# A wait-driven attention and feed-forward kernel: one load queue, a split transform, folds behind the first slots, norms on three engines, flat scans

## The reference, cut to what matters

```python
# x: (8, 128, 256), ctx: (8, 128, 256), T = 128 steps, C = 256 channels
def step(carry, kv_t):                    # _wkv, scanned over the 128 steps
    p, q, o = carry
    no = jnp.maximum(o, u + kt); A = jnp.exp(o - no); E = jnp.exp(u + kt - no)
    y = (A * p + E * vt) / (A * q + E)
    ...                                   # p, q decay by exp(w) and take in exp(kt)*vt, exp(kt)
x = x + jnp.tanh(g_xattn[0]) * _wkv(w, u, _layernorm(x), ctx)
h = fwht(_layernorm(x) * SU_ug) / 64      # Walsh-Hadamard transform over 256
h = silu(h @ W_gate.T * s_gate) * (h @ W_up.T * s_up)         # inner width 1024
h = fwht(h * SU_dp) / 64                  # over 1024
x = x + jnp.tanh(g_ffn[0]) * (h @ W_down.T * s_dp)
```

## Time and profile before

| | before |
|---|---|
| time, median of 3 runs | 117.35 us (116.47 to 118.0) |
| time of the profiled execution | 116.77 us |
| its span, first to last instruction | 115.0 us |
| TensorE busy | 98.3 us, 85% |
| VectorE, ScalarE, GpSimd busy | 70.3, 67.5, 61.4 us |
| TensorE's share of the chain that ended last | 71% |
| mean granted TensorE clock | 0.996 |

### The profile page before, as it was taken

The page is one execution under the profiler, slowest core; times in us unless marked ns, Lnnn a source line. Parts: engine busy times, 40 slices in busy tenths (PEclk is TensorE's granted clock), DMA queues, the critical chain, the costliest instruction groups (busy, mean ns, idle before and its releaser), DMA issues.

```text
span 115.0 us, 1940 instructions
## 1 busy us (share of the span) xinstructions
PE 98.3 (85%) x684; PEld 88.9 (77%) x684; DVE 70.3 (61%) x145; ACT 67.5 (59%) x146; POOL 61.4 (53%) x76
## 2 busy tenths in 40 slices
PE   0027778899799999999999999999999999779990
PEld 0026555756489969699999999999999999679870
DVE  0399899908996795997996475972219611322211
ACT  4299675044699907999525899373659723405400
POOL 7022999799759897942432734624402542312420
PEclk9999999999999999999999999999999999999998
DMA  3899998000000000000000020000020000020002
GB/s 65 267 324 415 418 404 350 0 0 3 3 6 0 0 0 0 0 0 6 0 0 3 6 91 0 0 0 0 6 91 0 3 0 6 0 91 0 3 1 90
DMA packets 3036, 7.62 MB, mean 66 GB/s; under 512 B 465, under 2 KB 850, under 8 KB 2898
## 3 DMA queue, kind: packets, MB, share of 16 engines
q1 hardware_dynamic: 2880, 7.48, 17.7%
q10 hardware_dynamic: 146, 0.02, 0.1%
HBM read 6.45 MB, written 1.05 MB: 65 GB/s over the span
## 4 chain that ended last, share of the span: by engine, by line
PE 71%; DVE 15%; ACT 4%; DMA 4%; issue 2%; POOL 1%; POOLq 1%; DVEq 0%; ACTq 0%
PE UG L899 38%; PE OD L937 12%; PE KZ L937 6%; PE UG L826 5%; PE FX L858 5%; DMA X<-in_x 4%; DVE X L327 2%; PE FX L867 2%; DVE BS L667 1%; DVE XT L761 1%; PE VB L875 1%; DVE SP_ L639 1%; DVE SQ L639 1%; ACT S L595 1%; DVE DEN L697 1%
## 5 line engine op out<-in xcount | busy, mean ns | idle before, releaser
L458 POOL TENSOR_TENSOR HL<-H,HH 128x256 fp32r<-128x256 f32 x32 | 25.8, 814 | 32.3 <-ACT HH L586 32.3
L775 DVE SCALAR_TENSOR_TENSOR H<-S,ALPHA,UG 128x256 f32<-128x256 f32 x32 | 15.0, 478 | 22.3 <-ACT S L595 22.2
L595 ACT ACTIVATE S<-UG,VT 128x256 f32<-128x256 f32 x32 | 15.1, 473 | 17.5 <-PE UG L899 17.5
L899 PE MATMUL UG<-FH,WTH 128*128 128x256 f32 x128 | 21.4, 289 | 0.8 <-ACT FH L580 0.8
L899 PE MATMUL UG<-FL,WTH 128*128 128x256 f32 x128 | 20.4, 281 | 0.0
L899 PE MATMUL UG<-FH,WTL 128*128 128x256 f32 x128 | 20.3, 280 | 0.0
L899 PEld LDWEIGHTS UG<-FH,WTH 128*128 128x128 f32 x128 | 17.8, 188 | 2.1 <-issue 1.9
L899 PEld LDWEIGHTS UG<-FH,WTL 128*128 128x128 f32 x128 | 17.4, 188 | 0.0
L899 PEld LDWEIGHTS UG<-FL,WTH 128*128 128x128 f32 x128 | 17.3, 188 | 0.0
L586 ACT ACTIVATE HH<-H 128x256 fp32r<-128x256 f32 x32 | 13.2, 413 | 4.5 <-DVE H L775 4.2
L937 PE MATMUL OD<-HH,MH 128*128 128x256 f32 x40 | 11.3, 283 | 1.6 <-DVE XT L761 1.6
(11 more groups left out here) (120 smaller groups left out, 200.3 us busy)
## 6 DMA issues: line engine op xcount, KB each, us to landing
WN<-in_weights SPq DMA_DIRECT2D x4, 512.0 KB, 9.1
DN<-in_w_down SPq DMA_DIRECT2D x1, 1024.0 KB, 8.1
out<-XT SPq DMA_DIRECT2D x3, 256.0 KB, 2.5
V<-in_ct SPq DMA_DIRECT2D x2, 258.0 KB, 7.7
V<-in_ct SPq DMA_DIRECT2D x1, 516.0 KB, 12.1
X<-in_x SPq DMA_DIRECT2D x2, 256.0 KB, 4.7
XT<-in_xt SPq DMA_DIRECT2D x2, 256.0 KB, 8.6
X<-in_x SPq DMA_DIRECT2D x1, 512.0 KB, 10.9
```

The costliest lines, as they stand in the source:

```text
L458: pool.tensor_tensor(HL[:, q % JT, 0:n], ring(H, q), HH[:, q % JT, 0:n].bitcast(F32), ALU.subtract).then_inc(h_lo, 1)
L595: act.activation(ring(S, q), gate_part(q), ACT.Silu, scale=VT[:, V_SGATE + j:V_SGATE + j + 1]).then_inc(silu_ready, 1)
L775: dve.scalar_tensor_tensor(out=ring(H, q), in0=ring(S, q), scalar=ALPHA[:, j:j + 1], in1=up_part(q), op0=ALU.mult, op1=ALU.mult).then_inc( ...
L899: return pe.matmul(dst.rearrange("p (g n) -> p g n", n=GT), w[:, m, j, t, :], f[:, chunks, t, :], start=start, stop=stop, skip_group_check ...
```

## The change

- **Loads**: the constants, the sign-turned Hadamard block and the small vectors are one transfer HI on SP's queue; ACT issues no load. x of group 1 comes ahead of the context, x of groups 2 and 3 ahead of the second halves of the weights. The padded column of V is gone.
- **Split transform**: for group 0 `fwht` becomes `x_part` (AT times XT, as loaded) and `y_part` (AT times YT, the gated attention output), both into FX. The sum XT + YT is made later on GpSimd (`x1_first`, slot 4). The centring of AT is four products and one ScalarE copy in place of two products and two VectorE subtractions.
- **Folds behind the first slots**: `m` 0 to 3 all stand in slots 2 to 4 and write to KZ and VB. `m_rest` is gone; `m_lo` is a VectorE subtraction in slots 0, 1, 2 and 4. `LAG` is 6, not 4.
- **Norms on three engines**: keys of group 0 are normalised on VectorE, 1 and 3 on GpSimd, 2 on ScalarE (before: 0 and 1 on VectorE, 2 and 3 on GpSimd).
- **Flat scans**: all groups scan 512 elements over the one decay tile D0 and clear three elements after it; the padded decay tile D is gone.
- A stage `warm`, products that nobody reads, is written but stands in no table, so none is issued.

```diff
-LAG = 4
+LAG = 6
 PE_STAGES = {
-    -1: [("keys", 0), ("center", 0), ("w", 0), ("w_rest", 0), ("w", 1), ("w", 2), ("w", 3), ("w_rest", 1), ("w_rest", 2), ("w_rest", 3),
-        ("keys", 1), ("fwht", 0), ("m", 0), ("ones", 0), ("keys", 2), ("m", 1), ("m_rest", 0)],
+    -1: [("keys", 0), ("w", 0), ("center", 0), ("w_rest", 0), ("x_part", 0), ("w", 1), ("w", 2), ("keys", 1),
+        ("w_rest", 1), ("w", 3), ("y_part", 0), ("w_rest", 2), ("ones", 0), ("w_rest", 3), ("keys", 2)],
...
 ACT_STAGES = {
...
-    5: [("m_lo", 2), ("exp_block", (("rstd2", 1), ("recip", 2))), ("m_hi", 3), ("f_hi", 1)],
+    5: [("exp_block", (("recip", 2), ("rstd2", 1))), ("f_hi", 1)],
...
 POOL_STAGES = {
...
-    4: [("error", 2)],
+    4: [("x1_first", 0)],
+    6: [("error", 2)],
...
+                elif name in ("x_part", "y_part"):
+
+                    if name == "x_part":
+                        pe.wait_ge(at_ready, 1)
+                        pe.wait_ge(xt_in[0], 16)
+                    else:
+                        pe.wait_ge(y_ready, 1)
+                    for t in range(CT):
+                        for o in range(CT):
+                            i = pe.matmul(FX[:, o * GT:(o + 1) * GT], AT[:, o, t, :].bitcast(F32), XT[:, 0, t, :] if name == "x_part" else YT[:, t, :],
+                                          start=(name == "x_part" and o == t == 0), stop=(name == "y_part" and t == CT - 1), skip_group_check=True)
```

More of the change, by code:

```diff
@@ L55 @@
 ACT_STAGES = {
[L56 to L60, removed]
-    5: [("m_lo", 2), ("exp_block", (("rstd2", 1), ("recip", 2))), ("m_hi", 3), ("f_hi", 1)],
-    6: [("m_lo", 3)],
+    -1: [("setup", 0), ("own", 0), ("decay", 0), ("keys", 0), ("ratio", 0), ("signs", 0), ("w_hi", 0), ("center", 0), ("recip", 0), ("w_lo", 0), ("w_hi", 1),
+        ("w_hi", 2), ("w_lo", 1), ("w_hi", 4), ("keys", 1), ("w_hi", 3), ("w_hi", 5), ("square", 0), ("rstd2", 0), ("norm1", 2), ("f_hi", 0),
+        ("w_lo", 2), ("keys", 2), ("w_lo", 3), ("recip", 1), ("keys", 3)],
+    0: [("m_hi", 0)],
+    1: [("m_hi", 1), ("w_hi", 6)],
+    2: [("m_hi", 2), ("w_hi", 7)],
+    4: [("square", 1), ("m_hi", 3)],
+    5: [("exp_block", (("recip", 2), ("rstd2", 1))), ("f_hi", 1)],
     9: [("x_hi", 2)],
     11: [("square", 2)],
-    12: [("exp_block", (("rstd2", 2), ("recip", 3))), ("f_hi", 2)],
+    12: [("exp_block", (("recip", 3), ("rstd2", 2))), ("f_hi", 2)],
     17: [("x_hi", 3)],
@@ L130 @@
 X_HI = places(ACT_STAGES, "x_hi")
-M_FULL, M_REST = (places(PE_STAGES, n) for n in ("m", "m_rest"))
+M_FULL = places(PE_STAGES, "m")
 SHARED = ("norm1", "av", "error", "w_lo", "m_lo", "fly", "x_lo")
@@ L216, in build @@
[L216 to L222, removed]
+        steps_set, plus_clear, pads, d_clear, half, eps_set, ones_set, own_set = (sem(n) for n in (
+            "steps_set", "plus_clear", "pads", "d_clear", "half", "eps_set", "ones_set", "own_set"))
@@ new lines, in build @@
+        tanh_gate, decay_low, c_ready, m_ready, ratio_ready, decay_set, alpha, outs = (sem(n) for n in (
+            "tanh_gate", "decay_low", "c_ready", "m_ready", "ratio_ready", "decay_set", "alpha", "outs"))
+        signs, wplus, steps_r, centers, at_ready = (sem(n) for n in (
+            "signs", "wplus", "steps_r", "centers", "at_ready"))
+        filled, m_full, m_hi, w_full, w_hi, w_left, ni_ready = (sem(n) for n in (
+            "filled", "m_full", "m_hi", "w_full", "w_hi", "w_left", "ni_ready"))
@@ L791, in stage @@
             def stage(name, g):
-                if name == "keys":
+                if name == "warm":
+                    pe.wait_ge(ones_set, 1)
+                    for _ in range(g):
+                        pe.matmul(VB[:, 0:WARM].rearrange("p (k q) -> p k q", q=P), ONES[:, :], ONES[:, :].unsqueeze(1).broadcast_to([P, WARM // P, P]),
+                                  start=True, stop=True)
+                elif name == "keys":
                     if g == 0:
@@ L870, in stage @@
                 elif name == "ones":
-                    if g:
+                    if g == 1:
+                        pe.wait_ge(squared, CT + 1)
+                        wait_shared(pe, "m_lo", *M_FULL[1::2])
+                        for t in range(CT):
+                            i = pe.matmul(VB[:, 0:GT], ONES[:, :], FSQ[:, t, :], start=(t == 0), stop=(t == CT - 1))
+                    elif g:
                         pe.wait_ge(e_ready, 3 * g)
-                        pe.wait_ge(summed, g)
+                        pe.wait_ge(summed, g - 1)
                         i = pe.matmul(VB[:, 0:GT], ONES[:, :], FSUM[:, :], start=True, stop=True)
```

279 lines of the change are left out of this document (147 added, 132 removed).

## The result

The changed kernel takes 122.44 us (median of 4 executions, 122.01 to 122.99) against 116.91 us (median of 4, 116.41 to 118.0) of the kernel before: ratio 1.046, interval 1.036 to 1.056. It is slower. The profiled execution took 122.84 us, against 116.77 us of before.

What follows compares the result with a forecast made beforehand. After one long dependence up to slot 0, almost only TensorE was taken to bound the kernel, with a nearly slackless ScalarE and VectorE chain behind slot 5. 116.77 + 3.4 + 0.7 = 120.9, with 1.7 for the clock 122.6 us; range 118 to 127.

Steps and rivals of the forecast that it cites:

- XL half: Second half of group 2's transform on TensorE, which reads XL: predicted to start 3.4 us later than before.
- end: Behind the last `up`: two more down pairs stand there with LAG 6, predicted +0.7 us, bounds 0.7 and 1.4.
- clock: TensorE's granted clock falls behind the stall at group 2's transform: predicted +1.7 us, between 0 and 2.5.
- second chain: ScalarE, VectorE and GpSimd work behind slot 5, up to XL of group 2: predicted 4 us longer.
- The start: Everything up to slot 0's first product: predicted 3.9 us earlier, at 26.9, bounds 23.6 and 30.4.
- The slots up to 5: Slot 0 to the end of `up(5)`: predicted 18.4 us, using up the earlier gain and ending at 45.3.
- the thin stretch: 21.2 to 26.9 us, where TensorE has some 2.3 us of products: predicted to cost nothing for the clock.
- the collision of FL with GpSimd: Between slot 0 and `up(5)`: the prediction counted a wait for FL of 0.4 us.
- Rival 4: The chain to XL has slack and only TensorE's work counts: 116.1 us, down to 112.8; chance 0.17.
- Rival 3: The clock never rises ahead of slot 0, which starts at 30.4: 127 us; chance 0.13.
- Rival 2: The same waits, but the clock is kept: 119.5 to 122 us, centre 120.9; chance 0.2.

Runs made afterwards that it cites:

- e12: The kernel before, with its two small loads moved from ScalarE's queue to SyncE's, behind x of group 0: 116.71 us, ratio 1.000.
- e5: The changed kernel with `error` earlier on GpSimd, scan and `estimate` earlier on VectorE, and unread products ahead of keys of group 2: 115.85 us, ratio 0.986.
- e9: e5 plus separate free banks (KZ and FX) for the last group's down sums: 114.27 us, ratio 0.979.
- e1: The changed kernel with `error` of group 2 moved on GpSimd from slot 6 back to slot 4: 118.05 us, ratio 1.007.
- e3: The changed kernel with the edits of both e1 and e2: 117.82 us, ratio 1.004.
- e2: The changed kernel with VectorE's slot 5 reordered, scan ahead of `root` and `estimate` ahead of FL: 117.58 us, ratio 1.005.
- e10: The changed kernel with five unread products in slot 11, ahead of the split transform of group 2: 121.26 us, ratio unclear.
- e4: The changed kernel with five unread products on TensorE ahead of keys of group 2: 120.57 us, ratio 1.031.
- e7: The changed kernel with `LAG` 4 in place of 6: 122.48 us in the median, ratio unclear.
- e6: The changed kernel with one product per fold in place of two, leaving out half of the second transform: 118.99 us, ratio 1.015.

## Why the prediction was right, and what in it was not

The forecast of 122.6 us is 0.2 from the median of 122.44. By rows: predicted +3.4 (XL half), +0.7 (end), +1.7 (clock), together 5.8; measured 4.1 at the XL half and 2.0 in the tail, together 6.1. The forecast had `up(5)` where it ended before and gave all of the 3.4 to the second chain; measured, `up(5)` is 1.6 late and the second chain 2.5 longer. That the sums agree so well is luck, while the second chain is in both.

**The start.** Slot 0's first product came at 25.50, predicted 26.9: 1.4 us early. x of group 0 landed 0.7 us sooner than before (the chain's first piece is 3.43 us, and was 4.10), which I had not foreseen; e12 shows that the second queue had delayed it. And the clock rose near 15.2, some 2.4 us into `x_part` (an estimate from its 3.08 us, between the 3.78 of all slow and the 1.89 of all fast), not 5 us behind its start as I had taken from 20.41, so `y_part` started at 17.96, not 19.3. From the end of `ones` (22.09) to slot 0 it was 3.4 us, as said.

**The slots up to 5.** This is the step that failed in size. I counted 18.4 us from slot 0 to the end of `up(5)`, with no term for the clock in the thin stretch. It took 21.2 us. With no fall and no wait for FL of group 0 it took 18.3 (e5) and 18.2 us (e9), so the sum of products was right. With no fall and no filler it took 19.3 (e1) and 19.2 us (e3), of which 1.08 and 1.00 us are the wait for that FL, where I had counted 0.4. So the wrong terms are "nothing for the thin stretch", which measured 2.0 us (21.2 less 19.2, with a fall of 6.8 us), and the collision of FL with GpSimd, too small by some 0.6. Where the fall lasted 3.4 us, the stretch took 19.6 (e2) and 19.3 us (e10), so the short fall cost 0.4 at most. My argument, that VectorE sets the pace there, does not hold for what the long fall brings behind it: slots 0 and 1, in which TensorE is the bound. Slot 0 started 1.4 us early and 2.8 were lost, so `up(5)` ended at 46.73, not 45.3. With filler in that stretch e4 is 1.9 us faster in the median. An unforeseen gain hid half of the mis-sized terms.

**The second chain.** Right, in mechanism and nearly in size. Slot 8 waited 1.31 us for FH (predicted 1.5). VectorE waited 2.15 us for DEN ahead of `newton` (predicted: 2.0). XL ended at 65.65 (65.1). From `up(5)` to the XL half I had 19.8 us, and it was 19.0. (The XL half of before starts at 61.58, not at 61.75 as I had worked out from the chain's piece.) TensorE waited 0.80 + 1.95 = 2.75 us there, predicted 3.5. e1 and e2 took 1.9 and 2.2 us off this distance, and both together 3.1: less than their sum, as FH, and no longer XL, is the last wait of the middle. In the prediction `error` alone was given 2.0.

**The end.** +0.7 us predicted; 0.64 measured behind the last `up` (5.13 for 4.49), and e7 gives it back.

**The clock of the stall.** It fell, as forecast, and in each of the four executions, if the mean granted clock of 0.957 or 0.958 is read by the two falls of the profile. The price was 1.25 us, not 1.7 (1.1 to 1.8 by the tails: 52.57 against 51.47 in e6 and 50.78 in e10). But the waits alone do not bring the fall about: with the same waits the clock stayed up in the profiles of e6 and e7. I had the event and its size nearly right, and not its condition. The tail's 2.0 us are then these 1.25, the 0.64 of the end, and 0.36 that the same stretch takes longer when XL is waited for (3.22 us in e6, 2.86 before), less 0.3 in the slots between.

**The rivals.** Rival 4 was shown by e3 at its own mark: with XL in time the kernel was within 2% of before, 117.8 (I had given 116.1). Its condition did not hold in the changed kernel. Rival 3 did not occur in any profile. Rival 2, the same waits with the clock kept, is what the profiles of e6 and e7 show at the stall.

What stays open: why the clock fell around slot 0, and behind the stall, in some profiles and not in others. In e3 TensorE was busy for 1.87 us of the five from 21 to 26, in the changed kernel for 1.86 of the five from 20 to 25; the clock fell only in the latter, and the first rise had come later in the former. The Trainium skill, "TensorE: Matmul & The Clock Gate", section "What's actually happening", says that the moment of the rise varies from run to run, since the chip's watch over activity does not start with the kernel. The two `x_part` rows agree, 2.76 against 3.78 us for the same instructions. No run here shows whether the fall varies for that reason.

## What to carry to other kernels

Give every wait of the main engine two prices: the wait, and what the clock may lose behind it. Here the second was 1.25 us behind waits of 2.75 us, in the profiles where the clock fell, and 2.0 us behind a stretch in which the engine did little. It is a price with a chance: with the same waits the clock stayed up in two other profiles. A stretch where another engine sets the pace is not free of it, since the bill comes with the work behind it.

When work moves on the bounding engine, read the side chains as rods that hang on a point of its list: find the point, and measure the rod. Two stages moved in two tables, each hidden behind a wait that existed anyway, gave back 4.4 and 4.9 us of the 5.5 us that the redesign had lost; with filler in the thin stretch, a free bank for the last sums and one more order turned back, it came to 3% under the kernel before, of which the bank alone gives 2% in the kernel before.

## What was unexpected of the hardware

- The granted clock is listed as 1.00 from the start, at 12 to 16 us too, while the same eight records took 3.78 us (`x_part` in e3, 12.84) and 1.89 us (`y_part`, 19.20). Before the first rise the clock has to be read from durations.
- Between executions of one instruction sequence the first rise moved slot 0 from 25.30 (e10) to 26.73 us (e3). A difference of a microsecond between single profiles of this kernel means nothing unless `x_part` and the falls of the clock are compared too.
- One wait of 1.35 us (e1) and pauses of 1.57 us at the end left the clock at 1.00. Waits of about 1 us and 1.95 us with 0.7 us of products between them did so too in e6 and e7, and did not in the changed kernel and e4.
- The mean granted clock of an execution does not tell its time: of before's executions on one chip two took 116.55 and 116.37 us at 0.955, and one took 116.79 at 1.00; two of e10 took 118.92 us at 0.985 and 121.13 at 0.986.
- Twelve products of an `up` took 1.36 us in some stretches and 1.41 in others of one execution, both at a granted clock of 1.00 (e2: 1.36 for nearly all from 62 to 84 us, 1.41 from 85 on). I found no cause, and it moves the tails by up to 0.7 us.
- FL of group 0 took 1.69 us at 25.93, beside three additions of GpSimd that took 4.21 us, where FL of group 1 took 0.69 alone at 53.69.
